# Constant products of TensorE in the waits of a vision tower's block stages, and gate products with 40 rows

## The chip, the cores and the metric

The kernel runs on one core of a Trainium2 chip. The metric is the device time of one execution in microseconds (us). Engines: TensorE (PE; its weight loads are PEld), VectorE (DVE), ScalarE (ACT), GpSimd (POOL), SyncE (SP). All data are float32.

## The reference

A tokenizer (a Fourier neural operator with four layers) turns 128 images of 64x64x3 into 128 groups of 64 tokens with 64 features, 8192 tokens. Then come four levels of an attention-like and a feed-forward-like block, each `h = h + block(layernorm(h))`:

- L0: attention with a batch norm over all tokens (l0a, l0b), then a causal attention and a mixture of 8 experts, 2 chosen by a router (l0f)
- L1: attention with a relative bias (l1a), then 8 experts, the best one taken (l1f)
- L2: attention of 8 heads with rank 4 and an MLP (l2a), then a shared MLP and 4 experts, 2 chosen (l2f)
- L3: attention with a sigmoid, 8 heads (l3a), then 8 experts, 2 chosen (l3f)

The change touches no value of the result. A mixture needs `out[token] = sum over e of gate[token, e] * expert_e(token)`. With the experts' outputs held as features x tokens, each gate has to be spread over the 64 rows of its expert; a product with a matrix of zeros and ones does that.

## The kernel before, in words

The tokenizer runs first, and fills the first two thirds of the time. `build_blocks` (from L1468 on in the profile's lines) does the rest. It first runs l0a over all tokens, then a batch norm's sums, and then a loop of ITERS = 8 iterations. In each iteration two units (u = 0, 1) of 512 tokens go through the eight stages l0b, l0f, l1a, l1f, l2a, l2f, l3a, l3f.

Each stage has one function per engine: `l1f_tensor`, `l1f_scalar`, `l1f_vector` and so on. Every engine runs its own list in that written order. `p.need(who, step, u)` makes the engine wait for a step of another engine in the same stage, `p.done(...)` signals one. There is no planner and no tile framework; what stands behind a `need` in an engine's list waits too. TensorE has an explicit no-op behind each wait.

PSUM is held as `banks[u]`, four banks of 512 columns for each unit, named `B[u][bank]`. A stage that opens with a layer norm has VectorE compute moments, ScalarE a root, VectorE a reciprocal and two multiplications; TensorE then transposes the result (`stacked_tensor`, L1600, both units in one; `halves_tensor`, L1632, in l0f), ScalarE copies it to SBUF (`xT_stacked`), and the products follow (all through the helper `mm`, L1646, so that all products have this one line). The last transposes of a stage (`home_tensor`, L1621) bring the output back to tokens x features, and VectorE adds it to `h`.

Other waits of TensorE are for the softmax in l0f (L1996: transposes of the probabilities) and in l1a (L1724), and for the ranking of the experts in l0f (L2028: transposes of the gates). l0b (L1934) waits for ScalarE's relu of the batch norm.

The gates are spread by `share_tensor` in l1f and l3f and by the same lines written out in l2f. The gates of unit u lie in rows 32u to 32u+7 of a tile of 40 rows, `f_gT`, `m_gT` or `e_gT`; the rows between hold zeros, since `gates_stacked` (`gs`), from which they are transposed, is set to zero once. The product takes just the 8 (in l2f 4) rows of its unit. l0f has its own product of this kind (`expand`), which is not changed.

A product of float32 operands shows as two records in the profile, passes here; so `x4` on a line of the timeline is two products, or two for each unit when each is one pass of a pair.

Of the kernel before, what the change touches and what calls it, by code (L numbers as in the profile page):

```python
# [1197 lines left out]
def block_constants():  # L1198

    c = {}  # L1200
    c["eye"] = np.eye(128)
    c["eps"] = np.tile(np.array([[1e-5, 1e-11, 1e-10, 1e-6]]), (128, 1))
    c["mhalf"] = np.full((128, 8), -0.5)
    hd = 16
    inv_freq = 1.0 / 10000.0 ** (np.arange(0, hd, 2, dtype=np.float32) / hd)
    freqs = np.outer(np.arange(SEQ, dtype=np.float32), inv_freq)
    emb = np.concatenate([freqs, freqs], -1).astype(np.float32)
    sign = np.where(np.arange(hd) < hd // 2, -1.0, 1.0)
    cos, sin = np.cos(emb).T, np.sin(emb).T * sign[:, None]
    rows32 = lambda a, b: np.tile(np.concatenate([a, b], 0), (4, 1))  # L1210
    c["cos"], c["sin"], c["cossin"] = rows32(cos, cos), rows32(sin, sin), rows32(cos, sin)
    n = np.arange(128) % SEQ
    c["causal"] = np.where(np.arange(SEQ)[None, :] <= n[:, None], 0.0, -1e30)
    e = np.arange(8)
    c["before"] = np.tile((e[None, :] < e[:, None]).astype(np.float32).reshape(1, 64), (128, 1))
    e = np.arange(4)
    c["before4"] = np.tile((e[None, :] < e[:, None]).astype(np.float32).reshape(1, 16), (128, 1))
    own = np.zeros((8, NTILE * 128))
    for e in range(8):
        own[e, e * HID:(e + 1) * HID] = 1.0  # L1220
    c["expand"] = np.zeros((40, NTILE * 128))
    c["expand"][0:8], c["expand"][32:40] = own, own
    c["diag32"] = np.tile(np.kron(np.eye(8), np.ones((4, 32))), (4, 1))
    pairs = np.zeros((40, 4, 2, 64))
    for u in range(2):
        for e in range(8):
            pairs[32 * u + e, e // 2, e % 2] = 1.0
    c["pairs"] = pairs.reshape(40, 512)
    c["fold"] = np.tile(np.eye(64), (2, 1))
    return c  # L1230

# [228 lines left out]
def build_blocks(nc, tok, out_dram, weights_dram, consts_dram, where_w, where_c):  # L1460
    with ExitStack() as ctx:
# [3 lines left out]
        cst = sb("constants", [128, consts_dram.shape[1]])  # L1465
# [127 lines left out]
        rows = (lo, hi)  # L1593
        of = lambda ap, u, n=64: ap.rearrange("p (t c) -> p t c", t=T)[:, :, n * u:n * u + n]

        def stacked_tensor(p, tag, after):
            for u in R:
                p.need("dve", after, u)
            for t in range(T):
                last = nc.tensor.transpose(B[0][0][:, 128 * t:128 * t + 128], xs[:, t, :, :].rearrange("p u f -> p (u f)"),  # L1600
                                           eye)
            p.done_both(last)
# [105 lines left out]
        def attn_tensor(p, name):  # L1708
            p.need("act", "x.xT", 1)
            p.done_both(mm(B[0][1][:], W(name + "_q"), xTs[:]))  # L1710
            p.done_both(mm(B[0][2][:], W(name + "_k"), xTs[:]))
            for t in range(T):
                last = mm(B[0][3][:, 128 * t:128 * t + 128], xTs[:, 128 * t:128 * t + 128], W(name + "_v"))
            p.done_both(last)
            p.need("act", "q", 1)
            p.need("dve", "k", 1)
            for b in range(BATCHES):
                for u in R:
                    last = mm(B[1][u][rows[u], 64 * b:64 * b + 64], Q[0][rows[u], 64 * b:64 * b + 64],
                              K[0][rows[u], 64 * b:64 * b + 64])  # L1720
            p.done_both(last)
            p.need("dve", "p", 1)
            for t in range(T):
                last = nc.tensor.transpose(B[1][2][:, 128 * t:128 * t + 128], a_e[:, 128 * t:128 * t + 128], eye)  # L1724
            p.done_both(last)
            p.need("act", "pT", 1)
            p.need("dve", "v", 1)
            for t in range(T):
                for u in R:
                    for n, part in HALVES:  # L1730
                        last = mm(B[0][1 + n][rows[u], 64 * t:64 * t + 64], a_v[part, t, u, :],
                                  a_pT[part, t, 64 * u:64 * u + 64])
            p.done_both(last)
# [194 lines left out]
                a.done(nc.scalar.activation(Q[u][lo, :], Q[u][lo, :], ACT.Relu, bias=W("l0a_beta")), "y", u)  # L1928

        def l0b_tensor(p):  # L1930
            for u in R:
                p.need("act", "y", u)
                for t in range(T):
                    last = nc.tensor.transpose(B[u][0][:, 64 * t:64 * t + 64], Q[u][lo, 128 * t:128 * t + 128],  # L1934
                                               eye[lo, lo])
                p.done(last, "y", u)
# [21 lines left out]
        silu = lambda u, j: H[u][:, 1, :] if j % 2 else K[u][:]  # L1958
        gT = lambda u: tmp[u][32 * u:32 * u + 8, :]
        def l0f_tensor(p):  # L1960
            halves_tensor(p, "r", r, "r.out")
            for u in R:
                p.need("act", "r.xT", u)
# [16 lines left out]
            for u in R:  # L1980
                p.need("act", "v", u)
                p.need("dve", "k", u)
                for b in range(BATCHES):
                    o = slice(64 * (b % 2), 64 * (b % 2) + 64)
                    for g in range(4):
                        rows = slice(32 * g, 32 * g + 32)
                        c = at(b // 2) + 64 * (b % 2)
                        last = mm(B[u][g][o, 64 * (b // 2):64 * (b // 2) + 64], Q[u][rows, c:c + 64], K[u][rows, c:c + 64])
                p.done(last, "scores", u)
            for k in range(2):  # L1990
                for u in R:
                    if k == 0:
                        p.need("dve", "p", u)
                    for m in range(4):
                        t, i = 2 * k + m // 2, m % 2
                        last = nc.tensor.transpose(B[u][k][:, 128 * m:128 * m + 128],  # L1996
                                                   f_e(u)[:, 4 * t + 2 * i:4 * t + 2 * i + 2, :].rearrange("p g n -> p (g n)"),
                                                   eye)
                    p.done(last, f"pT{k}", u)
# [11 lines left out]
            for u in R:  # L2011
                p.need("act", "oT0", u)
                p.need("dve", "oT1", u)
                for t in range(T):
                    last = mm(B[u][1][:, 64 * t:64 * t + 64], o4(u)[:, 128 * t:128 * t + 128], W("l0f_wo"))
                p.done(last, "wo", u)
            halves_tensor(p, "f", r, "f.out")
            for u in R:
                p.need("act", "f.xT", u)
                for i in range(2):  # L2020
                    for n, part in HALVES:
                        last = mm(B[u][2 + n][:, 8 * i:8 * i + 8], x2(u)[part, 128 * i:128 * i + 128],
                                  W("l0f_router")[part, :])
                p.done(last, "logits", u)
            for u in R:
                p.need("dve", "gates", u)
                for t in range(T):
                    last = nc.tensor.transpose(B[u][3][0:32 * u + 8, at(t):at(t) + 128],  # L2028
                                               st[u][:, 160 + 8 * t - 32 * u:168 + 8 * t], eye)
                p.done(last, "gatesT", u)  # L2030
# [169 lines left out]


        def l1a_tensor(p):
            stacked_tensor(p, "x", "r.out")
            attn_tensor(p, "l1a")
            p.need("act", "oT", 1)
            for t in range(T):
                last = mm(B[0][0][:, 128 * t:128 * t + 128], a_oT[:, 128 * t:128 * t + 128], W("l1a_l"))
            p.done_both(last)
# [44 lines left out]

        def share_tensor(p, k, gT, bank):
            for u in R:
                p.done(mm(B[u][bank][:], W("pairs")[32 * u:32 * u + 8, 128 * k:128 * k + 128], gT[32 * u:32 * u + 8, :]),
                       f"share{k}", u)

        def sum_tensor(p, k, kept, bank):
# [16 lines left out]
        f_bank = lambda u, k: B[u][(3, 1, 2, 3)[k]]  # L2276

        def l1f_tensor(p):
            stacked_tensor(p, "x", "x.out")
            projected_tensor(p, "l1f_w1", "x", "hid")  # L2280
            for u in R:
# [86 lines left out]
            return dst(u)[part, k:T:2, 32 * rep:32 * rep + 32]  # L2368

        def l2a_tensor(p):  # L2370
            stacked_tensor(p, "x", "r.out")
            projected_tensor(p, "l2a_wx", "x", "hid")
            for u in R:
# [42 lines left out]
            for u in R:  # L2416
                p.need("act", "o0", u)
                p.need("dve", "o1", u)
                for t in range(T):
                    for a in range(2):  # L2420
                        last = mm(B[u][0][:, 64 * t:64 * t + 64], a2_o(u)[:, a, 128 * t:128 * t + 128],
                                  W("l2a_wo")[:, 64 * a:64 * a + 64], start=(a == 0), stop=(a == 1))
                p.done(last, "wo", u)
            stacked_tensor(p, "f", "f.out")
            projected_tensor(p, "l2a_w1", "f", "ff")
            for a in range(2):
# [128 lines left out]
        e_yT = A16[0][:, 512:1024]  # L2555

        def l2f_tensor(p):
            stacked_tensor(p, "x", "x.out")
            p.need("act", "x.xT", 1)
            for t in range(T):  # L2560
# [33 lines left out]
            p.need("dve", "gT", 1)  # L2594
            for k in range(2):
                for u in R:
                    last = mm(B[u][3 - 2 * k][:], W("pairs")[32 * u:32 * u + 4, 128 * k:128 * k + 128],
                              e_gT[32 * u:32 * u + 4, :])
                    p.done(last, f"share{k}", u)
            for k in range(2):  # L2600
                for u in R:
# [86 lines left out]
        y3 = A16[0][:, 3072:3584]  # L2688

        def l3a_tensor(p):  # L2690
            stacked_tensor(p, "x", "x.out")
            p.need("act", "x.xT", 1)
            for t in (1, 2, 3, 0):
# [114 lines left out]
        m_kept = lambda u, k: (Q[u][:], K[u][:], H[u][:, 0, :], H[u][:, 1, :])[k]  # L2808

        def l3f_tensor(p):  # L2810
            stacked_tensor(p, "x", "x.out")
            p.need("act", "x.xT", 1)
            for t in range(T):
# [225 lines left out]
```

How the kernel before makes its waits and increments, by code:

```python
        def sp_store_spectrum(sp, t):  # L236
            u = tile_buffer(t)
            sp.wait_ge(g_ready, t + 1)
            sp.wait_ge(zeroed, NZERO)
            if t == 0:
                sp.dma_start(grid_spec.rearrange("p r m -> p (r m)"), modes_out[u][0:6, :]).then_inc(x_stored[u], 16)
            else:
                sp.dma_start(spec_flat[128 * (t - 1):128 * t, :], modes_out[u][:]).then_inc(x_stored[u], 16)
# [3 lines left out]
        def sp_embed_loads(sp):  # L248
            sp.wait_ge(zeroed, 2)
            for s in range(2):
                sp.dma_start(inner[0][3 * s:3 * s + 2, :, :],
                             grid_rows[2 * s:2 * s + 2, :].rearrange("p (j w) -> p j w", w=COLS)).then_inc(tile_in[0], 16)
            sp.dma_start(eye[:], eye_dram).then_inc(basis_in, 16)
            for t in range(1, ET):
                sp.wait_ge(zeroed, 2 + t)
                sp.dma_start(inner[t], x_flat[128 * (t - 1):128 * t, :].rearrange("p (j w) -> p j w", w=COLS))\
                    .then_inc(tile_in[t], 16)
                if t == 1:
                    sp.dma_start(fwd[:], fwd_dram).then_inc(basis_in, 16)
# [1 line left out]
        def tile_loaded(eng, t):  # L262
            eng.wait_ge(tile_in[t], 32 if t == 0 else 16)
# [1 line left out]
        def sp_store_plane(sp, t):  # L265
            tile_loaded(sp, t)
            sp.wait_ge(zeroed, NZERO)
            if t == 0:
                sp.dma_start(grid_pad.rearrange("s k x -> (s k) x"), planes[t][0:6, :]).then_inc(pad_stored, 16)
            else:
```

## Time and profile before

| | us |
|---|---|
| median of 3 runs | 8684.14 (8684.07 to 8689.99) |
| the profiled execution | 8682.11 |
| its span | 8680.3 |
| TensorE busy | 7235.5 (83%) |
| VectorE busy | 5708.1 (66%) |
| ScalarE busy | 2199.0 (25%) |
| mean granted clock of TensorE | 0.905 |

The profile is of one execution. The granted clock is that of TensorE, as a share of 2.4 GHz. Busy times are unions over an engine's instructions; weight loads overlap products. The block loop is the stretch from 6017.87 to 8677.32 us after the span's start.

### The profile page before, as it was taken

The numbers are of one execution on the slowest core, as the hardware profiler recorded it, in microseconds if no ns is written. First come the engines' busy times: TensorE is split into PE (matmuls) and PEld (weight loads), VectorE is DVE, ScalarE is ACT, GpSimd is POOL, SyncE is SP. The second block draws the span as 40 slices with busy tenths as digits, with TensorE's granted clock in tenths as the row PEclk, the third lists the DMA queues.
The fourth block names the chain that finished last, engine by engine and source line by source line (L and its number), as shares of the span: only waits on it lengthen the run. The fifth ranks groups of instructions, "written<-read, shape, count | busy, mean of one in ns | idle before, by whom it ended". The sixth has DMA issues, their size and how long they took to land. (4 is left out here: it accounts for less than half of the span.)

```text
span 8680.3 us, 127373 instructions
## 1 busy us (share of the span) xinstructions
PE 7235.5 (83%) x40246; PEld 3613.7 (42%) x40246; DVE 5708.1 (66%) x11527; ACT 2199.0 (25%) x3710; POOL 48.9 (1%) x43
## 2 busy tenths in 40 slices
PE   6788886899999799999969999994766766767667
PEld 5544444544444554444453222223333333333333
DVE  4799995688888478888846777766454454454554
ACT  3211112211111221111122222212333333333333
POOL 0000000000000000000000000000000000000000
PEclk8999998999999799999989999996888788878788
DMA  7655557766666766666675444440000000000000
GB/s 216 139 122 126 124 121 174 203 176 180 182 180 178 202 192 180 181 178 178 183 211 140 120 120 120 120 111 33 1 3 3 1 3 3 1 3 3 1 3 2
DMA packets 641898, 957.77 MB, mean 110 GB/s; under 512 B 527656, under 2 KB 531312, under 8 KB 582902
## 3 DMA queue, kind: packets, MB, share of 16 engines
q1 hardware_dynamic: 641560, 953.49, 41.6%
q8 instruction: 184, 3.01, 0.2%
q14 instruction: 154, 1.26, 0.0%
HBM read 621.93 MB, written 344.28 MB: 111 GB/s over the span
## 5 line engine op out<-in xcount | busy, mean ns | idle before, releaser
L603 PE MATMUL abank<-inv_basis,mode_tile 128*128 128x512 f32 x2048 | 1017.4, 621 | 174.6 <-DMA mode_tile<-m_modes 164.7
L970 DVE TENSOR_TENSOR work<-inv_copy,abank 128x512 f32<-128x512 f32 x1024 | 657.0, 683 | 614.5 <-ACT inv_copy L845 614.2
L665 PEld LDWEIGHTS gbank<-fwd_basis,turned 128*128 128x128 f32 x6368 | 745.9, 193 | 369.3 <-issue 217.9
L665 PE MATMUL gbank<-fwd_basis,turned 128*128 128x128 f32 x6368 | 821.6, 282 | 51.6 <-ACT turned L853 51.6
L1001 DVE TENSOR_TENSOR arena<-zbank,work 128x512 f32<-128x512 f32 x1024 | 701.0, 685 | 207.8 <-PE zbank L638 207.7
L634 PE MATMUL zbank<-arena,conv_bd 128*64 128x512 f32 x3072 | 830.6, 619 | 3.0 <-DVE mixed L1159 2.2
L636 PE MATMUL zbank<-arena,conv_bd 128*64 128x504 f32 x3072 | 781.3, 587 | 0.0
L638 PE MATMUL zbank<-arena,conv_bd 128*64 128x504 f32 x3072 | 779.7, 586 | 0.0
L1003 DVE SCALAR_TENSOR_TENSOR arena<-arena 128x512 f32<-128x512 f32 x1024 | 708.5, 692 | 35.3
L853 ACT ACTIVATE turned<-tbank 128x512 f32<-128x512 f32 x796 | 432.0, 595 | 1103.0 <-PE tbank L652 1103.0
L603 PEld LDWEIGHTS abank<-inv_basis,mode_tile 128*128 128x128 f32 x2048 | 364.4, 196 | 539.8 <-issue 498.6
L652 PEld LDWEIGHTS tbank<-eye,work 128*128 128x128 f32 x3184 | 344.3, 141 | 370.2 <-issue 276.4
L845 ACT ACTIVATE inv_copy<-abank,conv_bias 128x512 f32<-128x512 f32 x256 | 175.9, 687 | 1242.4 <-PE abank L603 1242.4
L652 PE MATMUL tbank<-eye,work 128*128 128x128 f32 x3184 | 437.7, 281 | 53.4 <-DVE work L1027 36.3
L845 ACT ACTIVATE inv_copy<-abank 128x512 f32<-128x512 f32 x256 | 152.8, 597 | 1056.2 <-PE abank L603 1056.2
L802 PE MATMUL zbank<-mix_w,arena 128*128 128x128 f32 x1024 | 243.2, 413 | 207.5 <-DVE mix_w L1149 129.3
L1149 DVE SCALAR_TENSOR_TENSOR mix_w<-uv,twid,partial 128x512 f32<-128x512 f32 x256 | 181.0, 748 | 351.8 <-ACT partial L930 335.9
L636 PEld LDWEIGHTS zbank<-arena,conv_bd 128*64 128x64 f32 x3072 | 221.0, 137 | 440.4 <-issue 440.4
L638 PEld LDWEIGHTS zbank<-arena,conv_bd 128*64 128x64 f32 x3072 | 220.8, 137 | 429.7 <-issue 429.7
L1646 PE MATMUL banks<-xT_stacked,weights 64*128 64x512 f32 (+1 forms) x896 | 343.6, 829 | 41.2 <-ACT xT_stacked L1611 31.2
L868 ACT ACTIVATE modes_out<-tbank,q_bias 128x512 f32<-128x512 f32 x256 | 175.9, 687 | 789.3 <-PE tbank L729 789.3
L981 DVE TENSOR_TENSOR work<-work 128x512 f32<-128x512 f32 x512 | 352.2, 688 | 20.8
(341 smaller groups left out, 9070.6 us busy)
## 6 DMA issues: line engine op xcount, KB each, us to landing
h_rows<-arena SPq DMA_DIRECT2D x192, 1024.0 KB, 16.2
arena<-h_rows SPq DMA_DIRECT2D x192, 1024.0 KB, 6.1
arena<-h_rows SPq DMA_DIRECT2D x384, 496.0 KB, 8.7
m_modes<-mixed SPq DMA_DIRECT2D x64, 1024.0 KB, 6.8
mode_tile<-m_modes SPq DMA_DIRECT2D x512, 128.0 KB, 4.3
g_modes<-modes_out SPq DMA_DIRECT2D x192, 256.0 KB
arena<-x_slots SPq DMA_DIRECT2D x192, 194.9 KB
arena<-g_modes SPq DMA_DIRECT2D x36, 1024.0 KB, 11.1
```

Of the source, the lines that this page charges most:

```text
L603: last = nc.tensor.matmul(abank[px][:], mode_tile[u][:, 2 * px + k, :, :].rearrange("p a c -> p (a c)"), inv[:, 2 * px + k, :], start=True ...
L634: nc.tensor.matmul(out[a], conv_bd[:, 1, :], src[a], start=True, stop=False)
L636: nc.tensor.matmul(out[a][:, :, 1:COLS], conv_bd[:, 0, :], src[a][:, :, 0:COLS - 1], start=False, stop=False)
L638: last = nc.tensor.matmul(out[a][:, :, 0:COLS - 1], conv_bd[:, 2, :], src[a][:, :, 1:COLS], start=False, stop=True)
L652: last = nc.tensor.transpose(tbank[px][:, m:m + 128], folded[q][:, px, py, 128 * b:128 * b + 128], eye[:])
L665: last = nc.tensor.matmul(gbank[u][:, 128 * k:128 * k + 128], turned[q][:, k // 2, k % 2, b, :], fwd[:, 2 * q + b, k, :], start=(q == 0 an ...
L853: last = nc.scalar.activation(turned[q][:, px, :, :, :].rearrange("p y b n -> p (y b n)"), tbank[px][:], ACT.Identity)
L970: nc.vector.tensor_tensor(inverse[:, 2 * k + part, :], inv_copy[k][:], abank[1][:], op)\
L981: nc.vector.tensor_tensor(spectral[u][:, low, :, 0, :], base, delta, ALU.add)
L1001: nc.vector.tensor_tensor(out, zbank[o % 2][:], added, ALU.add).then_inc(z_full, 1)
L1003: nc.vector.scalar_tensor_tensor(out=out, in0=out, scalar=0.01, in1=out, op0=ALU.mult, op1=ALU.max)\
L1646: return nc.tensor.matmul(out, lhsT, rhs, start=start, stop=stop)
```

## The change

Three parts:

1. A function `fill(n, bank)` issues n products of 128x128 by 512 columns of the constants tile, into a PSUM bank that nothing reads before it is next written. It is called in 13 places of the block loop's TensorE lists, each ahead of a wait, 65 products an iteration. One of them, with 12 products, has a wait of its own ahead of it, for VectorE's step `masked0`, which reads the bank that it writes.
2. The products that spread the gates in l1f, l2f and l3f take all 40 rows of the gates' tile. Their matrices of zeros and ones are two now, `pairs0` and `pairs1`, with 40 rows each and zeros outside the unit's own rows.
3. The constants tile has 512 columns more for it.

```diff
-    c["pairs"] = pairs.reshape(40, 512)
+    pairs = pairs.reshape(40, 512)
+    none = np.zeros((32, 512))
+    c["pairs0"], c["pairs1"] = np.concatenate([pairs[0:8], none], 0), np.concatenate([none, pairs[32:40]], 0)
...
+        def fill(n, bank):
+            for _ in range(n):
+                mm(bank[:], cst[:, 0:128], cst[:, 0:512])
+
...
             p.done_both(last)
+            fill(6, B[0][1])
             p.need("dve", "p", 1)
...
         def l0b_tensor(p):
+            fill(1, B[0][1])
...
         def l0f_tensor(p):
+            fill(4, B[0][1])
             halves_tensor(p, "r", r, "r.out")
...
                     if k == 0:
+                        if u == 0:
+                            p.need("dve", "masked0", 0)
+                            fill(12, B[0][0])
                         p.need("dve", "p", u)
...
+            fill(2, B[0][2])
             halves_tensor(p, "f", r, "f.out")
...
                 p.done(last, "logits", u)
+            fill(6, B[0][0])
             for u in R:
                 p.need("dve", "gates", u)
...
         def l1a_tensor(p):
+            fill(4, B[0][0])
             stacked_tensor(p, "x", "r.out")
...
         def share_tensor(p, k, gT, bank):
             for u in R:
-                p.done(mm(B[u][bank][:], W("pairs")[32 * u:32 * u + 8, 128 * k:128 * k + 128], gT[32 * u:32 * u + 8, :]),
+                p.done(mm(B[u][bank][:], W(f"pairs{u}")[:, 128 * k:128 * k + 128], gT),
                        f"share{k}", u)
...
         def l1f_tensor(p):
+            fill(9, B[0][1])
             stacked_tensor(p, "x", "x.out")
...
         def l2a_tensor(p):
+            fill(5, B[0][2])
             stacked_tensor(p, "x", "r.out")
...
                 p.done(last, "wo", u)
+            fill(4, B[1][2])
             stacked_tensor(p, "f", "f.out")
...
         def l2f_tensor(p):
+            fill(4, B[0][0])
...
-                    last = mm(B[u][3 - 2 * k][:], W("pairs")[32 * u:32 * u + 4, 128 * k:128 * k + 128],
-                              e_gT[32 * u:32 * u + 4, :])
+                    last = mm(B[u][3 - 2 * k][:], W(f"pairs{u}")[:, 128 * k:128 * k + 128], e_gT)
...
         def l3a_tensor(p):
+            fill(4, B[0][0])
...
         def l3f_tensor(p):
+            fill(4, B[0][0])
```

The first call stands in `attn_tensor`, which l1a alone uses, behind the scores.

## Rows read from the trace of the kernel before

**Rows 1.** The page: span, TensorE's clock in tenths, and an eviction's group.

```profile
span 8680.3 us, 127373 instructions
...
PEclk8999998999999799999989999996888788878788
...
L853 ACT ACTIVATE turned<-tbank 128x512 f32<-128x512 f32 x796 | 432.0, 595 | 1103.0 <-PE tbank L652 1103.0
```

**Rows 2.** Windows: stretch, length, busy time by engine, clock, DMA: loop; l1f twice.

```profile
6017.87:8677.32 2659.45, 1837.14 (x14496) 949.57 (x14496) 1289.79 (x4008) 966.56 (x1655) 14.75 (x16) 0.80 0.01 2
...
7144.49:7183.54 39.05, 30.56 (x96) 11.56 (x96) 14.62 (x57) 14.55 (x23) 0.00 (x0) 0.89 0.00 1
...
6146.02:6186.80 40.78, 32.31 (x96) 11.76 (x96) 14.62 (x57) 14.55 (x23) 0.00 (x0) 0.83 0.00 1
```

**Rows 3.** Waits of TensorE in one iteration, 7015 to 7346: total us, times, longest.

```profile
PE banks L1600 <- DVE x_stacked L1545: 29.3, 6, 8.9
PE banks L1996 <- DVE big L2126: 10.9, 1, 10.9
PE banks L2028 <- DVE small L2154: 6.4, 1, 6.4
...
PE banks L1724 <- DVE big L1766: 5.8, 1, 5.8
PE banks L1934 <- ACT qt L1928: 4.6, 1, 4.6
PE banks L1600 <- DVE small L1555: 4.1, 1, 4.1
PE banks L1632 <- DVE r L1545: 3.6, 1, 3.6
...
PE banks L1632 <- DVE r L1579: 2.7, 1, 2.7
```

**Rows 4.** Timeline and window of l1a's and l1f's first transposes and products.

```profile
7117.99 1.08 PE L1600 MATMUL banks<-constants,x_stacked 128*128 128x128 f32 x4 [3.89 <-DVE x_stacked L1545]
...
7120.10 3.75 PE L1646 MATMUL banks<-xT_stacked,weights 128*128 128x512 f32 x4 [1.02 <-ACT xT_stacked L1611]
...
7149.77 3.76 PE L1646 MATMUL banks<-xT_stacked,weights 64*128 64x512 f32 x8 [0.84 <-ACT xT_stacked L1611]
...
7120.10:7123.60 3.50, 3.50 (x4) 1.48 (x5) 0.00 (x0) 0.69 (x1) 0.00 (x0) 0.50 0.00 0
```

**Rows 5.** Timeline and window of the later part of l1f.

```profile
7168.23 3.60 PE L1646 MATMUL banks<-hid,weights 128*128 128x512 f32 x8
...
7171.76 1.99 PE L1646 MATMUL banks<-big,constants 8*128 8x512 f32 x8
...
7182.12 0.63 PE L1621 MATMUL banks<-constants,big 128*128 128x128 f32 x4 [0.84 <-ACT big L2337]
...
7154.95:7182.70 27.75, 25.66 (x84) 9.54 (x84) 10.78 (x33) 8.85 (x14) 0.00 (x0) 1.00 0.00 1
```

**Rows 6.** Windows of stretches in l0f and at the end of l2f.

```profile
7055.29:7058.48 3.19, 2.96 (x20) 2.45 (x20) 0.38 (x2) 1.50 (x4) 0.00 (x0) 0.50 0.00 0
7044.43:7047.60 3.17, 3.12 (x14) 2.75 (x15) 1.04 (x2) 1.19 (x2) 0.00 (x0) 0.51 0.03 5
7047.60:7052.63 5.03, 4.68 (x148) 4.06 (x146) 3.04 (x5) 2.57 (x5) 0.00 (x0) 1.00 0.01 3
...
7256.90:7259.20 2.30, 1.91 (x8) 0.66 (x8) 2.25 (x4) 0.00 (x0) 0.00 (x0) 1.00 0.00 0
7259.48:7267.20 7.72, 6.74 (x14) 1.95 (x14) 1.04 (x2) 1.92 (x2) 0.00 (x0) 0.50 0.00 0
...
7064.90:7068.00 3.10, 3.10 (x14) 2.09 (x16) 0.00 (x0) 1.76 (x3) 0.00 (x0) 0.50 0.00 0
```

**Rows 7.** The DMA view: size and time to landing of the constants.

```profile
constants<-in_constants SPq DMA_DIRECT2D x1, 1358.0 KB, 5.7
```

## The prediction

> **What bounds the kernel now.** I read the page first, then one iteration of the block loop by windows, then what TensorE waited for in it, then single stretches of the timeline. The page [rows 1] gives a span of 8680.3 us and, in its row of TensorE's clock, 10 (full speed, 2.4 GHz) over nearly all of the tokenizer and 7 or 8 tenths in the last 13 slices, the block stages. The change is in those stages alone. They take 2659.5 us for 8 iterations, 332.4 each, with TensorE busy 1837 us of it at a mean granted clock of 0.80 [rows 2]. Granted are 1.00 or 0.50 only, so 0.80 means that 40% of the time, 133 us of an iteration, stands at the low level, 1.2 GHz.
>
> The waits [rows 3] show why. In one iteration TensorE sits idle 13 times for 2.7 us or more, always for VectorE's or ScalarE's short dependent steps (layernorm, softmax, ranking): at the transposes that open seven normalised inputs, five times about 4.1 and once 8.9 in the first row and 4.1 in the second, and at the other six rows. After such an idle stretch the clock is low: the first transposes and products of the stage run at 0.50 [rows 4, 6]. Then it rises, and the rest of the stage runs at 1.00. Stages are chains of transpose, eviction, product, eviction, so what TensorE loses there is mostly on the path.
>
> The same stage in two iterations gives the rate of exchange [rows 2]: l1f takes 39.05 us at a mean clock of 0.89 and 40.78 at 0.83, for the same instructions. That is 8.6 and 13.9 us at the low level: 5.3 us more cost 1.73, or 0.33 for each. TensorE is busy 78% of l1f and 69% of the whole, so 0.29 for the whole.
>
> **The added products.** A product of 128x128 with 512 columns is two passes. At 1.00 four of them take 3.60 us [rows 5], 0.86 each with the drain of the last set aside. At 0.50 two take 3.75 [rows 4], some 1.75 each. The change adds 65 of them an iteration: 1, 4, 12, 2 and 6 in l0b and l0f, 4 and 6 in l1a, 9 in l1f, 5 and 4 in l2a, 4 each in l2f, l3a, l3f. None has a reader. Each run stands ahead of a wait, and what is queued behind it on TensorE is just the transposes (or, once, products) that this wait holds. Against the waits [rows 3], at 1.00: 0.9 in 4.6; 3.4 in 3.6; 10.3 in 10.9; 1.7 in 2.7; 5.2 in 6.4; 3.4 in about 4.1 (l1a; in l2a, l2f, l3a, l3f too); 5.2 in 5.8; 7.7 in 8.9; and l2a's 4.3 in 4.1. So at full clock all are hidden but the last, which is 0.2 late. At 0.50 nearly all overrun (rival 1).
>
> **What they give back.** With the runs in place the idle pieces left before the transposes are 0.2 to 1.2 us, but for two places: l0b keeps 3.8, and between the wo products and the router's logits there is a chain of short pieces. Per iteration:
> - Transposes of one tile (four passes) take 1.08 at 0.50 and 0.63 at 1.00 [rows 4, 5]: 0.45 less. Seven at the inputs, the one of the scores in l1a, and the last of l2f are low now: 9 x 0.45 = 4.1.
> - Products. Eight passes in unit pairs take 3.76 at 0.50 and 1.99 at 1.00 [rows 4, 5]: 1.77 less; one full product 0.86 less. Low now are: in l1a q, k, v (2.6) and parts of scores, attended and projection (1.9); in l1f the first layer (1.8); in l2a three sets (5.3); in l2f the logits (0.8), s1 (0.9), two expert layers (1.8), the bias product and the down products (0.9 + 1.8); in l3a the v products, half of them at the rise (1.5); in l3f the logits and the first experts (2.9). Together 22.0. Evictions between them (0.6 us for each 512 columns, ScalarE's row of [rows 1]) come as fast as the products at full clock in l1f, l2a's MLP, l2f and l3f, so I take off 3: 19.0.
> - l0f's three low stretches: TensorE is busy 3.1 at the probabilities' transposes, 3.0 at the logits and 3.1 from the gates on [rows 6]. Half of each at most is saved; evictions and small weight loads leave 1.3, 0.9 and 1.4: 3.6.
> - l0b's transposes and the start of l0f I count at nothing: with 3.8 us idle left in l0b the clock will be low there, then the four products run partly low, and what they overrun (up to two products, 1.7, less 0.2 of slack) eats what the next products save (about 1.5). Bounds: -2 to +2.
>
> The sum is 26.7 an iteration. By the rate of exchange, 133 us less some 20 that stay low, times 0.29, is 33. I keep 26.7, which is counted.
>
> **The 40-row products.** Now u=0 and u=1 use rows 0 to 7 and 32 to 39 of the array, and four such products (eight passes) take 1.99 us [rows 5], half of what four 128-row products need: the two units run at once. With 40 rows, both from row 0, they can't, so each of the ten pairs of an iteration costs 0.86 more at 1.00. In l3f TensorE is all but continuous there: four pairs, less the half microsecond that the last one hides, 2.9. In l1f two short waits absorb a little: 2.8. In l2f VectorE's multiplications go on beside them: 0.8 of 1.7. Together 6.5; bounds 3 (half hidden) and 8.6 (nothing hidden). For it there is a gain already counted: in l2f the clock falls at the end of the 4-row products, though TensorE was busy 1.91 of those 2.30 us, and all that follows to the end of the stage, 7.7 us, is at 0.50 [rows 6]. The products of few rows seem to count little for the clock. In l1f the 8-row ones did no such harm: 1.00 all through [rows 5]; there the edit only costs.
>
> **The rest.** Places where the clock may still fall (after the scores of l0f, whose 12 products would then overrun by about 1 us; before the logits) I count at 1.2 lost, l2a's late run at 0.2. The constants grow by 512 columns, 256 KB; they are waited for once. 1358 KB landed in 5.7 us [rows 7], so 1.1 us, between 0 and 2, once.
>
> Sum: 26.7 - 6.5 - 1.4 = 18.8 an iteration, 150.4 for eight, less 1: 149. The profiled execution took 8682.1 us beside its span of 8680.3; from it 8533. The median of the runs is 2.0 above it: 8535.
>
> A rule of the Trainium skill speaks against this. TensorE: Matmul & The Clock Gate, Part 4 (PE-mode transpose), says that transposes don't count as TensorE work for the clock. The trace shows the contrary: at the probabilities of l0f only transposes ran from 7044.4 to 7047.6 and the clock rose from 0.50 to 1.00 at their end [rows 6]. If the rule held here, it would make rival 3.
>
> **Rivals.**
> 1. *Slower: the added products run at the low clock and come late.* At 0.50 throughout they overrun their waits by 3.3 + 9.7 + 0.8 + 3.9 + 3.0 + 4.5 + 6.6 + 4.5 + 2.9 + 3 x 2.7 = 47 us an iteration, and the shares cost double: 8 x 60, 9160 us, and the change would not do what it says. But the rows show that steady work raises the clock, so the real form is that each run starts low and turns full after a few products. It decides at about 20 us of overrun an iteration, 1.7 at each of twelve places. With three low products in each: 2.6 - 0.5 = 2.1 x 12 = 25, + 6.5 - 26.7 = +5, or 8720. For it: after the 2.7 us wait in l0f the clock was low. Against: most runs begin right behind stretches at 1.00 [rows 5]. 6%.
> 2. *Kept only in part.* Idle pieces of 1 to 3 us that remain round the transposes let the clock fall at half of the places; then half of 26.7, less 6.5: 6.9, 8630 us. 18%.
> 3. *Transposes count as idle.* Then from the end of a run to the first product some 2.5 us pass without work, as long as the wait after which l0f's logits were low [rows 6], and the products at the starts (15 of the 19 us) gain nothing: 26.7 - 15 - 7.9 = 3.8, 8654 us. This is the page's rule. 4%.
> 4. *More.* The rate of exchange is the truer one (33), half of the shares' cost is hidden: 33 - 3 - 1 = 29 x 8 = 230, 8455 us. 10%.
>
> The forecast itself has 60%, and 2% are left for no change. So faster by over 0.2% (17 us; less can't be told from no change here) 0.92, same 0.02, slower 0.06. The forecast's own range is 8490 to 8580, from the bounds of the shares and of l0f's start; to hold 8 in 10 it goes to 8455 below and, with most of rival 2, to 8615 above.
>
> **What would show it.** Right: the mean clock over the block loop at 0.93 or more from 0.80; the opening transposes at 0.63 us; each run ends before the step that its wait names, l2a's excepted; two 40-row products one after the other; l2f at 1.00 to its end; l1a and l2a shorter by some 5 and 6 us, l1f and l3f about as long as before; the tokenizer unchanged. Wrong: a run at 0.50 that ends after its wait, and a wait of VectorE or ScalarE for TensorE in its place; or opening products still at 0.50.

## The result, and the profile after

| | before | after |
|---|---|---|
| median | 8685.03 us (8684.07 to 8689.99, 4 runs) | 8573.44 us (8560.97 to 8593.79, 4 runs) |
| profiled execution, span | 8682.11, 8680.3 | 8581.94, 8580.1 |

The ratio is 0.9873 (95% interval 0.9851 to 0.9895): 112 us faster, where 149 were forecast. The changed kernel also spreads more, 33 us between its four runs in place of 6 (the kernel before spread by 12 to 21 us where it ran nine times, beside the experiments).

The page after, the rows that answer to [rows 1]:

```profile
PEclk8899998999999899999989999997999999998999
...
L1652 PE MATMUL banks<-constants 128*128 128x512 f32 x1040 | 526.4, 658 | 23.0 <-issue 23.0
```

The clock's row is at 9 nearly throughout the block stages. The added products are a group of their own: 65 products of 2 passes in 8 iterations are 1040 passes. Windows of the changed kernel: the loop, then l1a, l1f, l2a and l2f of its third iteration, then l1f of its sixth (stretch, length, busy time of each engine, clock, DMA):

```profile
6022.03:8577.18 2555.15, 2201.10 (x15534) 1086.54 (x15534) 1298.58 (x4008) 961.04 (x1655) 14.75 (x16) 0.94 0.01 2
...
6752.31:6778.96 26.65, 23.08 (x124) 12.31 (x123) 14.82 (x60) 7.19 (x13) 0.00 (x0) 0.89 0.00 1
6778.96:6818.11 39.15, 35.53 (x107) 13.88 (x106) 15.10 (x57) 14.44 (x23) 0.00 (x0) 1.00 0.00 1
6818.11:6861.29 43.18, 34.51 (x176) 22.06 (x175) 20.42 (x81) 20.27 (x40) 1.84 (x2) 1.00 0.00 1
6861.29:6896.42 35.13, 29.50 (x89) 10.70 (x89) 14.24 (x69) 11.76 (x22) 0.00 (x0) 0.81 0.00 1
...
7735.79:7783.46 47.67, 44.25 (x108) 16.33 (x108) 15.09 (x57) 14.44 (x23) 0.00 (x0) 0.81 0.00 1
```

Against [rows 2] the loop is 104.3 us shorter, at a mean clock of 0.94 in place of 0.80. l2a is at full clock; l1a and l2f are not. And l1f, which takes 39.15 us in one iteration, takes 47.67 in another. Waits of TensorE over the loop, after, for the steps of [rows 3] (total, times, longest):

```profile
PE banks L1652 <- issue: 32.8, 40, 3.6
PE banks L1942 <- ACT qt L1935: 27.3, 2, 26.5
PE banks L1606 <- DVE x_stacked L1547: 24.5, 41, 0.8
PE banks L1638 <- DVE r L1581: 7.1, 8, 0.9
PE banks L2042 <- DVE small L2168: 2.2, 2, 1.1
PE banks L2008 <- DVE big L2140: 1.8, 4, 0.5
```

L1606 is the opening transpose (L1600 before). It still waits up to 0.8 us in 41 of 56 cases; there the added products end in time. In 7 more, those of l2a, it starts 0.15 us after its input, as before. In 8 it is late: l1a in five iterations, and three places in the sixth and seventh. In l0b and l0f being late is the rule. L1942 waits in the first iteration (26.5 us, for the batch norm) and in the sixth. L1638 has waits on the later norm of l0f alone (L1581); at the opening of l0f it never waits. L2008 (the probabilities of l0f) waits in 2 of 8 iterations, twice in each, and L2042 (the gates) in the same 2: in the others the added products end after the step that they fill, and TensorE is late.

Mean over the eight iterations, from the ends of each stage's last addition to `h` in the two traces, in us. "Low" is the time of the stage after that stands at the clock of 0.50. "At full clock" is what the stage takes in the iterations in which it stands at 1.00 from end to end (l1a and l2f never do in this kernel; theirs are from e11 below).

| stage | before | after | saved | of the forecast | low | at full clock |
|---|---|---|---|---|---|---|
| l0b + l0f | 100.6 | 98.2 | 2.3 | 2.4 | 13.0 | |
| l1a | 29.3 | 26.2 | 3.1 | 5.4 | 5.2 | 24.9 |
| l1f | 39.9 | 40.3 | -0.3 | -1.3 | 2.3 | 39.2 |
| l2a | 49.1 | 43.4 | 5.7 | 5.2 | 0.3 | 43.2 |
| l2f | 35.4 | 33.5 | 1.9 | 5.5 | 9.8 | 29.0 |
| l3a | 40.8 | 39.7 | 1.1 | 2.0 | 1.3 | 39.1 |
| l3f | 37.4 | 38.2 | -0.8 | -0.3 | 3.4 | 37.0 |
| sum | 332.4 | 319.4 | 13.0 | 18.8 | 35.3 | |

The forecast's column splits its sum by stage, with the 3 us for evictions spread evenly over the four stages named and the 1.2 for falls of the clock in l0f; the rows add up to 0.1 more than 18.8 (for the reason, see the last point of the account below). The saving of 13.0 in eight iterations is 104. The loop starts 4.2 us later than before. That difference stands already where the transfer of the constants is issued (5853.98 us, 5849.80 before), so it is the tokenizer's, which no edit touches; in the profiled executions of the other kernels here that moment lies between 5847.5 and 5858.1. The larger constants do land 1.0 us later (1614 KB in 6.7 us), but l0a makes that up before the loop starts.

### The profile page after: what moved, and what is told of

It is laid out like the page before. It is cut to its first block and busy times, and to the rows that moved or that the text cites. A ratio compares the mean times of both kernels' runs of the same rounds, so it can differ in the third digit from the quotient of the medians.

```text
span 8580.1 us, 129477 instructions
## 1 busy us (share of the span) xinstructions
PE 7603.3 (89%) x41286; PEld 3752.6 (44%) x41286; DVE 5718.8 (67%) x11527; ACT 2193.5 (26%) x3710; POOL 48.9 (1%) x43
## 5 line engine op out<-in xcount | busy, mean ns | idle before, releaser
L1003 DVE SCALAR_TENSOR_TENSOR arena<-arena 128x512 f32<-128x512 f32 x1024 | 708.6, 692 | 35.4
L1652 PE MATMUL banks<-constants 128*128 128x512 f32 x1040 | 526.4, 658 | 23.0 <-issue 23.0
```

The lines of the kernel that those rows point to most:

```text
L1003: nc.vector.scalar_tensor_tensor(out=out, in0=out, scalar=0.01, in1=out, op0=ALU.mult, op1=ALU.max)\
L1652: return nc.tensor.matmul(out, lhsT, rhs, start=start, stop=stop)
```

## The experiments

All are compared with the kernel before on the same chip. Ratio with its 95% interval; the changed kernel's is 0.9873.

| run | median us | ratio |
|---|---|---|
| e1, added products, old gate products | 8572.14 | 0.9876 (0.9861 to 0.9891) |
| e2, 40-row gate products alone | 8725.29 | 1.0052 (1.0038 to 1.0066) |
| e3, 40 rows in l2f alone | 8570.10 | 0.9869 (0.9854 to 0.9884) |
| e4, one more product in l2f and l3f | 8559.16 | 0.9862 (0.9847 to 0.9878) |
| e5, 8 rows in l3f | 8554.90 | 0.9849 (0.9835 to 0.9862) |
| e6, 8-row pair and a full product | 8601.36 | 0.9905 (0.9890 to 0.9920) |
| e7, none added in l0b and l0f | 8563.30 | 0.9861 (0.9846 to 0.9876) |
| e8, four in l0b | 8574.33 | 0.9884 (0.9869 to 0.9899) |
| e9, gate products of 128 rows | 8527.79 | 0.9815 (0.9801 to 0.9828) |
| e10, without the first 1 + 4 | 8568.24 | 0.9852 (0.9835 to 0.9869) |
| e11, combined | 8493.65 | 0.9774 (0.9761 to 0.9788) |
| e12, combined, none in l0b and l0f | 8505.19 | 0.9790 (0.9776 to 0.9803) |

**e1 and e2: the two halves of the change.** e1 takes back the gate products' edit and keeps `fill`; e2 does the reverse.

> The added products stay, the gate products are as before (8 rows in l1f and l3f, 4 in l2f). Theory A: two 40-row products go one after the other and so last 0.86 us a pair longer, and they hold the clock no better than the 8-row pairs of l1f and l3f; l1f then falls from 39.2 to about 36.5 us, l3f from 38.2 to about 35, l2f may rise by 1 to 2 since its clock falls at the 4-row products: 8573 - 8 x 4.5, some 8535 us. Rival B: the 40 rows are what keeps the clock up in the second half of l1f, l2f and l3f; without them it falls there, and the time is 8590 us or more.

> No added products, the 40-row gate products alone. Theory A: they cost 0.86 us a pair where TensorE sets the pace: l1f and l3f longer by 2.8 to 2.9 us each, and l2f within 1 us of before: 8685 + 8 x 6, about 8735 us. Rival B: l2f gains 3 us as its end runs at the full clock, and the sum is near 8685 + 8 x 3, 8710 us or less.

e2 came near theory A (8725 us; 8735 expected, 8710 or less by rival B): 43 us slower than before. Alone, the 40 rows cost. By stage, from its trace against the one before: l1f 2.9 us longer, l2f 0.9, l3f 2.7, together 6.5 an iteration; the stages without such products moved too, l1a 0.7 and l2a 1.9 shorter, l3a 1.1 longer, with their falls of the clock. e1 did not come as A said: it is no faster than the change. Windows of e1, l1f and l3f of its fourth iteration:

```profile
7094.21:7133.81 39.60, 35.08 (x106) 12.84 (x105) 14.61 (x57) 14.44 (x23) 0.00 (x0) 0.91 0.00 1
7252.64:7287.23 34.59, 29.27 (x123) 9.78 (x121) 16.41 (x50) 15.41 (x25) 0.00 (x0) 1.00 0.01 1
```

l3f takes 34.6 in six of eight iterations and 35.3 on average, against 38.2 in the change, as A has it. But in l1f the clock now falls in the stretch of the 8-row products in all eight iterations, and the stage takes 39.6 to 42.5: there B is right. My sentence that the 8-row products "did no such harm" holds for the kernel before, in all of its eight iterations and not only in the one that was read; with the added products it no longer holds. Why the clock holds there in one kernel and falls in the other stays open. Added products and 40 rows are not two independent terms: e1 and the whole change come out the same.

**e3 and e5: which stage wants the 40 rows.** e3: 8 rows in l1f and l3f. e5: 8 rows in l3f alone.

> All added products; 40 rows in l2f alone, 8 rows in l1f and l3f. Theory A: l1f and l3f as in the run with the old gate products (36.5 and 35 us), l2f as after the change (33.5): 8573 - 8 x 6, about 8525 us. If l2f's 40 rows are no help to the clock, the run with the old gate products everywhere is as fast or faster than this one. Rival B: 8590 us or more, as the clock falls in l1f and l3f.

> The changed kernel with 8-row gate products in l3f alone. Theory C, formed after the first four runs: products of few rows let the clock fall where they stand close together (l1f, l2f), and 40 rows let it fall less often; in l3f they stand apart between full products, so there the 40 rows only cost. l3f then takes 35.3 us in place of 38.2 and the others stay: about 8550 us. Rival: the clock falls elsewhere for it, in l0b to l2f or in l3f itself, and the time stays at 8565 to 8575.

e3 is a miss for both theories: l3f 35.9 as A says, l1f 40.5 with falls in every iteration as B says, the time unchanged. e5 comes out at 8555, near the 8550 of theory C: l3f 35.8, l1f 39.2 in seven of eight iterations (45.6 in the other). But the other stages did not stay, as C had it: in the profiled execution, the slowest of its five, l2f took 35.5 in every iteration, 2.0 more than in the change. The two intervals overlap (0.9835 to 0.9862, and 0.9851 to 0.9895), so the 18 us are not shown.

**e6 and e9: rows or time.** e6 leaves the pairs as before and sets a full product ahead of each (`fill(1, B[0][bank])`). e9 keeps the order of the change, with more rows:

```diff
-    c["pairs0"], c["pairs1"] = np.concatenate([pairs[0:8], none], 0), np.concatenate([none, pairs[32:40]], 0)
+    for u in range(2):
+        c[f"pairs{u}"] = np.zeros((128, 512))
+        c[f"pairs{u}"][32 * u:32 * u + 8] = pairs[32 * u:32 * u + 8]
...
-            share_tensor(p, 0, f_gT, 0)
+            share_tensor(p, 0, A16[0][:, 0:512], 0)
...
```

> Gate products of 8 and 4 rows as before the change, and ahead of each pair one full 128-row product that nothing reads: the same time of TensorE as the two 40-row products in turn. Theory C: the clock goes by the rows at work as well as by the time; here it holds to the end of l1f, l2f and l3f: l1f 39.3 to 40, l2f 31, l3f 37.2, and about 8573 - 8 x 3.5, 8545 us. Rival: only the time that TensorE is occupied counts; then nothing changes against the 40-row products, 8573 us.

> The changed kernel with gate products of 128 rows: the matrices of zeros and ones have 128 rows, 8 of them in use, and the moving operand is all of the tile's rows. TensorE's time is that of the 40-row products. Theory D: the rows at work decide how such a product counts for the clock, and 40 of 128 are still few; with 128 the falls at the gate products of l1f and l2f go: l1f 39.2 in all iterations, l2f 30.5 to 32, 8573 - 8 x 3, some 8550 us. Rival: the falls come from the waits round the gate products, not from the rows; l2f then stays at 33.5 and the time at 8565 to 8575.

The other calls of l1f, and those of l2f and l3f, change in the same way. The added rows of the moving operand hold whatever the tile has there, and meet rows of zeros in the matrix.

e6 refutes theory C in the form in which it stood: 28 us slower than the change, where 28 faster were expected. The full product ahead delays the first gate product of each pair (l1f 40.6 at full clock, l3f 40.2 to 41.0). For the clock it did help in l1f, where it holds at the gate products in seven of eight iterations and in e1 in none; in l2f it falls all the same, in the four products or within 0.9 us behind them. e9 confirms theory D, by more than it said: 46 us faster than the change (some 23 expected), and the intervals are clear of each other. l2f is 3.4 us shorter, l1f 1.3, l3f 0.8. The four gate products of one l2f, with what follows: first the changed kernel, then e9.

```profile
6882.98 5.74 PE L1652 MATMUL banks<-big,constants 40*128 40x512 f32 x8 [0.94 <-DVE big L2691]
6888.52 1.91 PE L1652 MATMUL banks<-big,weights 40*128 40x512 f32 x2
6890.35 3.68 PE L1652 MATMUL banks<-hid,weights 128*64 128x512 f32 x8
```

```profile
7183.76 3.67 PE L1653 MATMUL banks<-big,constants 128*128 128x512 f32 x8 [0.94 <-DVE big L2692]
7187.36 1.12 PE L1653 MATMUL banks<-big,weights 40*128 40x512 f32 x2
7188.41 1.94 PE L1653 MATMUL banks<-hid,weights 128*64 128x512 f32 x8
```

Same columns, same count, same wait ahead; only the rows differ, and with them what data pass through the array, which these runs do not tell apart. With 40 rows the clock falls within the four, and they and what follows take 11.1 us; with 128 rows it stays, and the same takes 6.6. It is not one lucky iteration: in the changed kernel the clock falls within these four products in four of eight iterations and 0.6 to 0.9 us behind them in the other four, in e9 in none of eight. In e9 no fall stands in the second half of l1f, l2f or l3f in any iteration (l1f 39.0 in all but one, 39.2 there).

**e4: one more product.** It goes between the opening transposes and the logits.

```diff
             stacked_tensor(p, "x", "x.out")
+            fill(1, B[0][1])
             p.need("act", "x.xT", 1)
```

> The changed kernel with one more added product in l2f and in l3f, between the opening transposes and the logits, 0.86 us long beside an eviction of 0.84. Theory: the short fall of the clock 6 us into l2f and l3f (3.4 us in most iterations) comes from the idle piece and the small logits products there, and goes; l2f and l3f 0.9 us shorter each: 8573 - 8 x 1.5, about 8560 us. Rival: the fall stays or moves behind the gate products, and the time stays at 8573, or is 8580 by the two products' own time.

The fall 6 us into the stage is gone from all eight iterations of l2f and l3f. The one at l2f's gate products stays in all eight (6.8 us in seven of them, longer in the last), so the rival has a part in it. In the profiled run l2f took 32.1 and l3f 37.0 on average (33.5 and 38.2 in the change). 8559 as expected, but the intervals overlap.

**e7, e8, e10: the start of the loop.**

> The changed kernel without the 25 added products of l0b and l0f (1, 4, 12, 2, 6). By the steps of the prediction they save 3.6 us an iteration less 1.2 for falls of the clock: l0b and l0f back from 98.2 to about 100.6 us, and 8573 + 8 x 2.4, about 8592 us. Rival: what they save is eaten by late ends, and the time stays within 5 us of 8573.

> Four added products in l0b in place of one, 3.4 us in a wait of 4.6. Theory: the idle piece of 3.8 us left in l0b is what makes the clock fall there in every iteration, and the four products of l0f's start run partly low and end late; with four the clock holds, and l0b and l0f lose 1.5 to 2 us an iteration: about 8560 us. Rival: the four products themselves run low or late, 8573 us or more.

> The changed kernel without the first 1 + 4 added products, in l0b and at the start of l0f. Theory: behind the loop's branch TensorE issues nothing for 3.1 us, so the clock is low when they start, they take up to 6.5 us there, and the first transposes of l0f come 2 us late; without them l0b and l0f take about 96.2 us in place of 98.2: 8573 - 16, about 8557 us. Rival: what they cost they give back in the products behind them, and the time is 8573 within 5.

All three missed. Without the 25 products (e7), l0b and l0f took 3.0 us more an iteration (2.4 counted), yet the time was 10 us lower, not 19 higher: l1a took 25.2, l1f 39.3 and l2f 31.3 in place of 26.2, 40.3 and 33.5, from fewer falls of the clock. In e8 l0b grew by 3.8 us and l0f shrank by 1.4, so that the three more products cost more than they gave. The timeline of the changed kernel at the turn of the loop shows why they start late:

```profile
6970.99 0.63 PE L1627 MATMUL banks<-constants,pT 128*128 128x128 f32 x4 [0.84 <-ACT pT L2896]
...
6974.73 2.05 PE L1652 MATMUL banks<-constants 128*128 128x512 f32 x2 [3.10 <-issue]
...
6976.70 1.11 PE L1942 MATMUL banks<-constants,qt 64*128 64x64 f32 x8
...
6977.74 6.50 PE L1652 MATMUL banks<-constants 128*128 128x512 f32 x8
...
6980.84 0.98 DVE L1547 TENSOR_TENSOR r<-sq,small 128x256 f32<-128x256 f32 x2
...
6984.08 0.60 PE L1638 MATMUL banks<-constants,r 128*128 128x128 f32 x4
```

Behind the loop's branch TensorE issues nothing for 3.1 us here, and for 3.1 to 3.6 at all seven turns; before, this lay inside the wait of 4.6 [rows 3]. What fills that time the trace does not show. The one product starts late, at the low clock; the four of l0f take 6.5 us, and the transposes (L1638) start some 2 us late: VectorE has written their input, `r`, at 6981.82. Leaving these five out (e10) gave l0b and l0f back only 0.3 us, not 2: the products behind them then run low (the low stretch at the start of l0f's work lasts 10 to 14 us, in place of 7 to 10). That step of mine, "nothing, -2 to +2", holds.

**e11 and e12: the terms together.** e11: 128-row gate products in l1f and l2f, 8-row in l3f, e4's products, one more in l1a between the transposes of the probabilities and what follows, and none of the first 1 + 4.

> Put together: the changed kernel without the first 1 + 4 products, with 128-row gate products in l1f and l2f and 8-row ones in l3f, with one more added product behind the opening transposes of l2f and of l3f, and one behind the transposes of the probabilities in l1a. If the single terms add up (2 for the start, 2.6 for l3f, 1.0 + 2.0 for l1f and l2f, 1.0 for l1a): 8573 - 8 x 8.5, about 8505 us. If a saving in one place moves the falls of the clock to another, no more than half of it: 8540 us.

> The combined kernel without l0f's other added products (12, 2 and 6); so none is left in l0b and l0f. In the changed kernel, leaving out all 25 made the time no longer (8563 against 8573), though l0b and l0f took 3.0 us an iteration more. Theory: that was made up by fewer falls of the clock in l1f and l2f, by the moments at which the stages then came; in the combined kernel these stages have next to no falls left, so the 3.3 us of l0f show: 8494 + 8 x 3.3, about 8520 us. Rival: the 20 products do not pay at all, and the time is 8494 or less.

e11 is the fastest, 199 us below the kernel before on the same chip and 80 below the change. l2f takes 29.0 and l1a 24.9 in every iteration, both at 1.00:

```profile
7144.26:7173.28 29.02, 24.23 (x91) 9.28 (x91) 14.24 (x70) 11.77 (x22) 0.00 (x0) 1.00 0.00 1
7037.22:7062.12 24.90, 21.93 (x128) 11.33 (x127) 14.83 (x61) 7.34 (x13) 0.00 (x0) 1.00 0.00 1
```

It is some 12 us below the sum of the single terms. e12 is 12 us slower than e11, between the two expectations of 26 and 0, and the intervals overlap. l0f took 95.4 us without its 20 products and 92.7 with them, and l1f, l3a and l3f gave back 1.4 in the profiled runs. So that they pay is likely and not shown; that e7 was no slower comes from the other stages.

## Why the prediction came out as it did

- **The mechanism** was right: the clock in the loop went from 0.80 to 0.94, the opening transposes take 0.6 us, and from l1a on the products at full clock fit the waits. l2a, where the clock holds, saved 5.7 us against some 5.2 counted.
- **The term that was mis-sized is the falls of the clock that remain.** I wrote "some 20 that stay low" and took off 1.2 us, all of it for l0f. It is 35.3 us, 13.0 of it in l0b and l0f. The rest lies in l1a (at its last products), in l2f (at the logits, and for 3 to 10 us at or just behind the gate products), in l3f (at the logits) and, in some iterations, in l1f and l3a. Taken as the mean of a stage less what it takes at full clock (the table), these falls cost 1.3 us in l1a, 1.0 in l1f, 0.2 in l2a, 4.5 in l2f, 0.6 in l3a and 1.2 in l3f: 8.8 an iteration, where the forecast had nothing for these six stages. At full clock throughout, the six would have saved 19.5, which is 3.1 more than the 16.4 counted for them. The difference, 5.7, is nearly all of the 5.8 that are missing. So one error made good a third of another, and that the time came within 38 us of the forecast is in part luck. e11 put products and rows in just these places, and l1a and l2f, then at 1.00 throughout, took 24.9 and 29.0: they saved 4.4 and 6.4, against 5.4 and 5.5 of the forecast. So only 1 us of l1a's term was too much by itself.
- **The 40-row products, cost.** Two go in turn and no longer together, as I had it. Two of them in l1f of the changed kernel, on the timeline, take what four took before ([rows 5], 1.99):

```profile
6808.90 1.98 PE L1652 MATMUL banks<-big,constants 40*128 40x512 f32 x4
```


The run e2 gives 43 us for eight iterations, 5.3 each, against 6.5 counted. In the three stages it is the 6.5 counted; the difference lies in stages that have no such product. In l1f, though, 0.9 of the 2.9 is clock: the iterations of before with a low stretch as long as in e2 take 40.8, and e2's take 42.8.
- **The 40-row products, gain.** Wrong for l2f: "at 1.00 to its end" did not come. The clock fell at the gate products or within 0.9 us behind them in all eight iterations, in the third for 10 us. e9 shows that 40 rows were too few here.
- **l2a's run of five** ended in time in seven of eight iterations: the transposes start 0.15 us after their input, as they did before. It was expected 0.2 late.
- **Rival 3**, transposes count as idle, had 4% and 8654 us. It did not come: l2a stands at 1.00 from its opening transposes on, with an idle piece behind them, in seven of eight iterations. Behind it stood the rule of the Trainium skill (TensorE: Matmul & The Clock Gate, Part 4, PE-mode transpose) that transposes don't count as TensorE work for the clock. The trace of before contradicts it: after the idle 10.9 us only transposes ran for 3.2 us, and then the clock rose from 0.50 to 1.00 [rows 6].
- **Rival 1**, late at the low clock, is real in l0f: its runs of 4, 12 and 6 ended some 1, 1.2 and 0.4 us late in the third iteration, and the run of 4 some 2 us late in the fourth, so the sign "each run ends before the step that its wait names" failed there. It decides nothing in the sum: l0b and l0f saved 2.3 against 2.4.
- **Rival 2**, kept only in part (6.9 an iteration, 8630 us), is as near as the forecast: 13.0 lies halfway between 6.9 and 18.8. The clock did fall again at many places, but at logits, gate products and last products, and not at the idle pieces round the opening transposes, which rival 2 had in mind.
- **Slips in the working.** The terms of the products add up to 22.2, not 22.0. The bounds of the shares and of l0f's start give 8568 as the upper end of the forecast's own range, not 8580, and the result lies above that. The page's row shows at most 9, "90% or more", where I wrote 10, and one of the last 13 slices is a 6.

What stays open: why the falls come where they do in a given iteration. The same stage ran 39.15 or 47.67 us with the same instructions; e7, e8 and e10 moved falls in stages that they don't touch. So differences under some 15 us between these kernels are not explained by their edits. Some 10 us of such differences can lie in the tokenizer, as the start of the constants' transfer shows.

## What to carry to other kernels

Where a chain of short dependent steps lets TensorE's clock fall, products without a reader in the waits give it back, if they end before the wait does; here that was 1.3%, and 2.3% with the places closed that were still open. Count the time that remains at the low clock before you book the gain, and look at several iterations, not one. When a product must be made with few rows, compare three forms: few rows beside each other, few rows in turn, and all rows with zeros in the matrix.

## What the hardware showed that I had not expected

- Four products of 512 columns with 128 rows, in turn, kept the clock at 1.00 in eight of eight iterations; with 40 rows, in the same place and of the same length, it fell within them or up to 0.9 us behind them in eight of eight, and in the iteration shown they took 5.74 us in place of 3.67.
- Behind the loop's branch TensorE issues nothing for 3.1 to 3.6 us. It costs nothing while a wait covers it; an instruction put at the head of the loop does not start sooner.
- Kernels whose clock falls at other moments in each iteration can have times that spread: 33 us over four runs of the change, 42 in e10, but 10 in e9. The kernel before spread by 6 over four runs and by 12 to 21 over nine. That the falls cause the spread is likely and not shown.
